# Setup of a graph and expert kernel: half-size row buffers, column sums on two engines, scaling on the way out of PSUM

## The reference

```python
def _L0_gnn_ref(H, W, A):
    HW = einsum('bnf,fo->bno', H, W)
    A_norm = relu((A + A.T) * 0.5)
    D = sum(A_norm, axis=1)
    D_safe = where(D > 0, D, 1.0)
    d_inv_sqrt = where(D > 0, D_safe ** (-0.5), 0.0)
    DAD = d_inv_sqrt[:, None] * A_norm * d_inv_sqrt[None, :]
    L_norm = eye(N) - DAD
    return relu(einsum('nm,bmo->bno', L_norm, HW))

x = x + _L0_gnn_ref(_layernorm(x, axis=-1), L0_gnn_W, adj)
x = x + _L0_ffn_ref(_layernorm(x, axis=-1), router_w, w1, b1, w2, b2)
```

## Time and profile before

| | |
|---|---|
| median of 3 runs | 950.52 us |
| profiled execution, its own time | 949.63 us |
| its span | 947.9 us |
| TensorE busy, share of the span | 94% |
| VectorE | 68% |
| ScalarE | 55% |
| GpSimd | 33% |
| granted TensorE clock, mean | 0.986 of full |
| HBM traffic over the span | 235 GB/s |

### The profile page before, as it was taken

The page is one execution under the profiler, slowest core; times in us unless marked ns, Lnnn a source line. Parts: engine busy times, 40 slices in busy tenths (PEclk is TensorE's granted clock), DMA queues, the critical chain, the costliest instruction groups (busy, mean ns, idle before and its releaser), DMA issues.

```text
span 947.9 us, 15352 instructions
## 1 busy us (share of the span) xinstructions
PE 890.9 (94%) x4446; PEld 724.9 (76%) x4446; DVE 645.9 (68%) x1558; ACT 516.9 (55%) x899; POOL 311.3 (33%) x312
## 2 busy tenths in 40 slices
PE   4766799999999999999999989999999999999997
PEld 3765588888888788878888857777777777777775
DVE  3996634756867734152424288888888888888886
ACT  3665332344443321222122287888888888888885
POOL 0689335555574734474433430000000000000000
PEclk9997899999999999999999999999999999999999
DMA  9983255676485336867766774777777777777771
GB/s 286 327 253 125 98 202 212 255 270 215 166 290 175 102 139 251 281 245 262 267 246 239 286 253 163 263 265 266 267 269 270 270 270 270 270 270 270 270 269 45
DMA packets 93022, 222.98 MB, mean 235 GB/s; under 512 B 8856, under 2 KB 59568, under 8 KB 81072
## 3 DMA queue, kind: packets, MB, share of 16 engines
q1 hardware_dynamic: 86752, 211.59, 63.3%
q0 software_dynamic: 2560, 8.39, 2.3%
q10 hardware_dynamic: 3664, 2.43, 1.0%
HBM read 157.89 MB, written 64.49 MB: 235 GB/s over the span
## 4 chain that ended last, share of the span: by engine, by line
PE 81%; DVE 7%; POOL 4%; issue 4%; ACT 3%; DMA 1%; DVEq 0%; ACTq 0%; POOLq 0%
PE bank L913 11%; PE bank L915 11%; PE bank L914 11%; PE bank L1290 6%; PE bank L1293 6%; PE bank L1277 6%; PE bank L1279 6%; PE bank L1278 6%; PE bank L1291 6%; POOL col_sum L543 3%; PE bank L858 2%; PE bank L330 2%; DVE y_lo L699 2%; PE bank L1299 1%; PE bank L1287 1%
## 5 line engine op out<-in xcount | busy, mean ns | idle before, releaser
L1367 DVE TENSOR_TENSOR gated<-c_all,act_h 128x512 f32<-128x512 f32 x256 | 177.7, 694 | 46.2 <-ACT act_h L1329 41.6
L1329 ACT ACTIVATE act_h<-bank,b_sb 128x512 f32<-128x512 f32 x256 | 176.5, 690 | 58.5 <-PE bank L1279 54.0
L1372 DVE TENSOR_TENSOR g_lo<-gated,g_hi 128x512 fp32r<-128x512 f32 x256 | 175.7, 686 | 0.2
L1336 ACT ACTIVATE g_hi<-gated 128x512 fp32r<-128x512 f32 x256 | 159.1, 621 | 4.4 <-DVE gated L1367 4.4
L1262 POOL DMA_DIRECT2D out<-fin x32 | 24.3, 759 | 367.6 <-DVE fin L1380 362.9
L913 PE MATMUL bank<-y_hi,stage 128*128 128x512 f32 x256 | 111.3, 435 | 3.6 <-DVE y_lo L699 3.6
L1002 POOL TENSOR_TENSOR rstd<-var_eps,neg_half 128x4 f32<-128x4 f32 x32 | 48.8, 1525 | 179.5 <-DVE var_eps L1039 179.4
L1277 PE MATMUL bank<-z_e,w_hi 128*128 128x512 f32 x256 | 103.8, 406 | 1.7 <-ACT act_h L1329 1.5
L913 PE MATMUL bank<-y,stage 128*128 128x512 f32 x256 | 104.5, 408 | 0.0
L1293 PE MATMUL bank<-g_lo,w_hi 128*128 128x512 f32 x256 | 101.0, 395 | 2.9 <-DVE g_lo L1372 2.9
L1290 PE MATMUL bank<-g_hi,w_lo 128*128 128x512 f32 x256 | 103.7, 405 | 0.0
(11 more groups left out here) (118 smaller groups left out, 1582.1 us busy)
## 6 DMA issues: line engine op xcount, KB each, us to landing
c_all<-c_scratch SPq DMA_DIRECT2D x64, 1024.0 KB, 8.0
s_scratch<-stage SPq DMA_DIRECT2D x14, 2048.0 KB, 8.4
stage<-s_scratch SPq DMA_DIRECT2D x14, 2048.0 KB, 7.8
z_e<-z_scratch SPq DMA_DIRECT2D x32, 512.0 KB, 7.0
z_scratch<-z_hl SPq DMA_DIRECT2D x31, 512.0 KB, 2.7
x_raw<-in_x SPq DMA_DIRECT2D x32, 256.0 KB, 7.8
x_res<-in_x SPq DMA_DIRECT2D x32, 256.0 KB, 7.1
r_e<-res_scratch SPq DMA_DIRECT2D x32, 256.0 KB, 2.7
```

The costliest lines, as they stand in the source:

```text
L1329: act.activation(v.act_h[e % R][:, :], ps_h[e % 2][:, :], ACT.Gelu, bias=v.b1_sb[:, e:e + 1]).then_inc(gelu_done, 1)
L1336: act.activation(v.g_hi[e % R][:, :], v.gated[e % R][:, :], ACT.Copy).then_inc(hi_done, 1)
L1367: dve.tensor_tensor(out=v.gated[e % R][:, :], in0=v.c_all[s][:, e, :], in1=v.act_h[e % R][:, :], op=ALU.mult).then_inc(gated_done, 1)
L1372: dve.tensor_tensor(out=v.g_lo[e % R][:, :], in0=v.gated[e % R][:, :], in1=v.g_hi[e % R][:, :].bitcast(FP32), op=ALU.subtract).then_inc(lo ...
```

## The change

1. **Buffers.** The last eight steps use half-size buffers: each of the three sets is cut in two, so that there are six for steps 8 to 15. `FREED_BY` names the step whose sum frees a buffer. Before, the load of step 11 waited for the sum of step 8, that of step 15 for the sum of step 13; now they wait for the sums of steps 6 and 9.
2. **Column sums.** GpSimd adds rows down to j = 5 only. The rows 4 to 1 enter a column's sum as more products with the column of ones on TensorE. Each of the three parts of the degrees has its own PSUM bank.
3. **Projections.** Jobs 0 to 3 are kept and scaled as before, but in steps 0 to 2. From job 4 on, ScalarE scales on the way out of PSUM, four 128x128 pieces a job, each with its own scale. The power -0.5 is taken for each step's jobs. Two PSUM banks take turns for the projections of the first half, and ScalarE does `keep` behind the relus of a step, not ahead of them.
4. **Variance.** `x_var` is made by a TENSOR_REDUCE over the variance and a constant in a third column, where a TENSOR_SCALAR was.
5. **Order at the end.** The first four `y_high`/`y_low` (m = 15 to 12) go into steps 14 and 15. The staging of unit 1's row goes between the remaining ones, ahead of the graph stage. Its four turned groups stand behind blocks 4, 7, 11 and 14 of unit 0, where they stood behind 2, 4, 10 and 13.

```diff
-    ps_x, ps_p = v.banks[4], v.banks[5]
+    ps_x, ps_p = v.banks[4], [v.banks[5] if k % 2 or k >= v.MB else v.banks[3] for k in range(v.U)]
...
-        dve.tensor_scalar(v.x_var[:, k, :], v.x_mv[:, :, 1], v.EPS, None, ALU.add).then_inc(x_var_done, 1)
+        dve.tensor_reduce(out=v.x_var[:, k, :], in_=v.x_mv[:, :, 1:3], axis=AX.X, op=ALU.add).then_inc(x_var_done, 1)
...
-        elif k <= MB:
+        elif k < MB:
+            wait(pe, hw_kept, k - 1)
+        elif k == MB:
             pe.wait_ge(hw_kept, k)
...
     def keep(act, k):
         _, m = place(k)
         act.wait_ge(hw_done, k + 1)
-        act.activation(v.hw0[:, m, :], ps_p[:, :], ACT.Copy).then_inc(hw_kept, 1)
+        if k < KEPT_RAW:
+            act.activation(v.hw0[:, m, :], ps_p[k][:, :], ACT.Copy).then_inc(hw_kept, 1)
+        else:
+            act.wait_ge(x_rstd_done, k + 1)
+            for q in range(Q):
+                last = act.activation(v.hw0[:, m, q * P:(q + 1) * P], ps_p[k][:, q * P:(q + 1) * P], ACT.Identity,
+                                      scale=v.x_rstd[:, k, q:q + 1])
+            last.then_inc(hw_kept, 1)
...
-    SET = [r % 3 if r < 12 else 1 + r % 2 for r in range(MB)]
+    SET = [r % 3 if r < 8 else 3 + (r - 8) % 6 for r in range(MB)]
+    HALVES = [(2, 0), (2, 1), (0, 0), (0, 1), (1, 0), (1, 1)]
+    FREED_BY = [None, None, None, 0, 1, 2, 3, 4, 5, 5, 6, 6, 7, 7, 8, 9]
+    low = low + [v.low[i][:, h * N // 2:(h + 1) * N // 2] for i, h in HALVES]
+    up = up + [v.up[i][:, h * MB // 2:h * MB // 2 + MB // 2 - 1, :] for i, h in HALVES]
...
+    LAST = 5
+    EARLY_AT = ((15, 14), (13, 12))
+    EARLY = 4
+    SECOND_AT = (7, 5, 3, 0)
...
-    ps_d = v.banks[7]
+    ps_d = [v.banks[2], v.banks[7], v.banks[4]]
...
         for r, j in enumerate(ROWS):
-            if 1 <= j <= MB - 2:
+            if r < 4:
+                pr.invert(pool, jobs(r))
+            for k in jobs(r - 1):
+                if k < pr.KEPT_RAW:
+                    pr.scale_kept(pool, k)
+            if 4 <= r < 12:
+                pr.invert(pool, jobs(r))
+            if LAST <= j <= MB - 2:
                 add_columns(j)
-            if r in (2, 4, 8, 12):
-                first = 4 * (2, 4, 8, 12).index(r)
-                pr.invert(pool, range(first, first + 4))
-            if r == 9:
+            if r == 10:
                 root(0)
-            if r in (10, 11, 12, 13):
-                for k in range(2 * (r - 10), 2 * (r - 10) + 2):
-                    pr.scale_kept(pool, k)
             if r == 14:
                 root(1)
         root(2)
-        for k in range(8, MB):
-            pr.scale_kept(pool, k)
...
+            for k in jobs(r):
                 if k:
                     pr.keep(act, k - 1)
-            for g in range(n_groups(j)):
-                relu(r, j, g)
...
+            if r >= 14:
+                for m in EARLY_AT[r - 14]:
+                    y_high(m)
-        for m in range(MB - 1, -1, -1):
+        for m in range(MB - 1 - EARLY, -1, -1):
             y_high(m)
+            if m == 10:
+                st.high_direct(act, 1)
+            if m in SECOND_AT:
+                st.high_group(act, 1, SECOND_AT.index(m))
...
             if k <= MB - 3:
-                pe.wait_ge(col_added, 14 - k)
+                pe.wait_ge(col_added, 14 - max(k, LAST - 1))
...
+            for j in range(LAST - 1, k, -1):
+                if j == k + 1:
+                    pe.wait_ge(relued, until_row(j))
+                last = pe.matmul(out, s_tri[:, block(j, k), :], v.one_col[:, :], start=False, stop=(j == k + 1))
...
-            if ahead and i in S_AT and S_AT.index(i) < st.n_groups(u + 1):
-                st.turn_group(pe, u + 1, S_AT.index(i))
+            s_at = S_AT if u else (4, 7, 11, 14)
+            if ahead and i in s_at and s_at.index(i) < st.n_groups(u + 1):
+                st.turn_group(pe, u + 1, s_at.index(i))
```

More of the change, by code:

```diff
@@ L364, in project_program @@
     pr.scale_kept, pr.scale_by_d, pr.turn_x, pr.copy_x, pr.project = scale_kept, scale_by_d, turn_x, copy_x, project
-    pr.keep, pr.scale, pr.high, pr.low = keep, scale, high, low
+    pr.keep, pr.scale, pr.high, pr.low, pr.wait_scaled = keep, scale, high, low, wait_scaled
     return pr
@@ L451, in setup_stage @@
 def setup_stage(nc, sem, v):
-    E, MB, CW, Q = v.E, v.MB, v.CW, v.Q
+    E, MB, CW, Q, N = v.E, v.MB, v.CW, v.Q, v.N
     low, up, s_tri, ident = v.low, v.up, v.s_tri, v.ident
-    low_in = [sem(f"low_in{i}") for i in range(3)]
-    up_in = [sem(f"up_in{i}") for i in range(3)]
+    low_in = [sem(f"low_in{i}") for i in range(9)]
+    up_in = [sem(f"up_in{i}") for i in range(9)]
     consts_made = sem("consts_made")
@@ L511, in sync @@
             s = SET[r]
-            before = [i for i in range(r) if SET[i] == s]
             for k in jobs(r):
                 pr.load(sp, k)
-            if before:
-                sp.wait_ge(summed, first_group[before[-1] + 1])
+            if r >= 3:
+                sp.wait_ge(summed, first_group[FREED_BY[r] + 1])
             sp.dma_start(low[s][:, 0:(j + 1) * P], v.adj[j * P:(j + 1) * P, 0:(j + 1) * P]).then_inc(low_in[s], 16)
@@ L592, in scalar @@
                 pr.copy_x(act, k)
+            for g in range(n_groups(j)):
+                relu(r, j, g)
+            for k in jobs(r):
                 if k:
                     pr.keep(act, k - 1)
-            for g in range(n_groups(j)):
-                relu(r, j, g)
             if r == 12:
@@ L683, in degrees @@
             dve.wait_ge(col_done, MB - a)
-            dve.tensor_tensor(out=v.deg_raw[:, a:b], in0=ps_d[:, a:b], in1=v.deg_row[:, a:b], op=ALU.add).then_inc(deg_step, 1)
+            dve.tensor_tensor(out=v.deg_raw[:, a:b], in0=ps_d[p][:, a:b], in1=v.deg_row[:, a:b], op=ALU.add).then_inc(deg_step, 1)
             dve.wait_ge(deg_step, first + 2)
@@ L720, in vector @@
                 degrees(1)
+            if r >= 14:
+                for m in EARLY_AT[r - 14]:
+                    y_low(m)
         degrees(2)
-        for m in range(MB - 1, 2, -1):
+        for m in range(MB - 1 - EARLY, -1, -1):
             y_low(m)
-        outward()
-        for m in range(2, -1, -1):
-            y_low(m)
+            if m == 10:
+                st.diagonal(dve, 1)
+                st.low_direct(dve, 1)
+            if m in SECOND_AT:
+                st.low_group(dve, 1, SECOND_AT.index(m))
+            if m == 3:
+                outward()
     stage = Plan()
@@ L974, in scalar @@
                 evict(u - 1)
-            if ahead:
+            if ahead and u:
                 st.high_direct(act, u + 1)
@@ L984, in scalar @@
                         copy_gate(w)
-                if ahead and g < st.n_groups(u + 1):
+                if u and ahead and g < st.n_groups(u + 1):
                     st.high_group(act, u + 1, g)
@@ L1111, in vector @@
                 mid(u - 1)
-            if ahead:
-                if u == 0:
-                    st.diagonal(dve, 1)
+            if ahead and u:
                 st.low_direct(dve, u + 1)
             for g in range(4):
-                if ahead and g < st.n_groups(u + 1):
+                if u and ahead and g < st.n_groups(u + 1):
                     st.low_group(dve, u + 1, g)
```

37 lines of the change are left out of this document (23 added, 14 removed).

## The result

The changed kernel takes 940.19 us (median of 4 runs, 935.79 to 941.07) against 950.07 of before in the same runs (948.55 to 951.11): ratio 0.9888 [0.9854, 0.9922], so it is 10 us faster. The forecast was 935.5. The profiled execution has 940.29 us for its own time and a span of 938.6; the forecast's sum for it was 935.0, so 5.3 us are missing.

A forecast was written before the change was run, and what follows sets the result against it. Unit 1's start bounds the kernel: TensorE is gapless behind it. Moving it from 112.4 to 97.8 us (6.4 earlier start, 8.2 shorter unit 0) takes 14.6 off 949.6: 935.0, stated 935.5; own range 930.5 to 938.5, with rivals to 942.

The forecast's parts named there:

- The frame: From unit 1's start on, TensorE works without a gap, so whatever moves that start moves the end by as much.
- GpSimd late for job 15: Rival in setup: GpSimd's nine powers at 1.6 us each delay job 15, +3.5 us, 939 us; chance 0.13.
- a low clock all through unit 0: Rival in unit 0: TensorE's clock stays low throughout, 7.1 us more, 942.5 us; chance 0.09.
- The load order is the same and DMA is full, so the transposes of step 10 stay at 63.8 us: Setup up to step 10: TensorE's transposes start no later than before, at 63.8 us.
- TensorE's added column sums run in its idle time: Setup: column sums moved from GpSimd to TensorE cost no time; unit 0 starts at 81.5 instead of 87.86 us.
- Steps 11 to 15: End of setup: sums of steps 11 and 12 start at 68.8 instead of 71.29 us; last relu at 81.4.
- x_var: VectorE's variance in setup: 0.18 us as a TENSOR_REDUCE, where it took 1.70 at 61.57 us.
- The low parts' pace: VectorE's low parts: 0.69 us each instead of 1.14, since GpSimd has nothing left to do.
- The stop: TensorE's 5.06 us stop in unit 0, waiting for unit 1's staging, goes; counted in the 8.2 us from unit 0's length.
- Unit 0's length: Unit 0 takes 16.3 us instead of 24.5, a gain of 8.2 us.
- The half-size buffers: Loads of rows 11 to 13 land earlier, worth 1.2 us; rival that nothing is gained: 936.7 us, inside the own range.
- the pace: Rival in setup: GpSimd's powers at nearly 3.00 us add 17 us to its line, kernel slower at 952 us; chance 0.04.

The follow-up runs named there:

- e3_last3: The changed kernel with GpSimd summing rows down to j = 3 instead of 5: 936.19 us, ratio 0.9850.
- e1_keep_ahead: The changed kernel with ScalarE keeping the projections ahead of a step's relus again: 938.24 us, ratio 0.9877.
- e2_raw8: The changed kernel with jobs 0 to 7 kept unscaled ahead of the relus and GpSimd scaling jobs 4 to 7 in step 12: 937.54 us.
- e12_after_last1: The changed kernel with GpSimd summing the columns of all rows and TensorE adding none: 935.92 us, ratio 0.9854.
- e10_x_var: The kernel combining e2_raw8 and e3_last3, with the variance made by a TENSOR_SCALAR again: 938.88 us, ratio 0.9895.
- e9_raw16: The kernel combining e2_raw8 and e3_last3, with jobs 8 to 15 also kept unscaled and scaled by GpSimd behind its last root: 938.38 us.
- e8_late_staging: The kernel combining e2_raw8 and e3_last3, with all high and low parts behind the rows and unit 1 staged in unit 0 again: 937.94 us.
- e4_old_sets: The changed kernel with the old three full-size buffer sets in all 16 steps: 940.14 us, ratio 0.9903.

## Why the prediction was right or wrong

The frame, the sign and the range (930.5 to 942) held; the forecast's own range, up to 938.5, did not. That the range held is in part luck: it reached to 942 for two rivals, GpSimd late for job 15 and a low clock all through unit 0, and neither came; what took the 4.7 us between forecast and median was none of the rivals that I had named. The gain by place is wrong too. Of the 14.6 us forecast, 6.4 were to come from unit 0's earlier start, and nothing did (87.86 us before, 87.92 now); 8.2 were to come from its length, and 9.0 did. Of the signs named for a right forecast, the first product near 81.5 and the eviction at 97 to 99 us failed. Two steps failed, and together they are the missing 5.3 us.

- **"The load order is the same and DMA is full, so the transposes of step 10 stay at 63.8 us": failed, +3.3 us in the profiled execution.** I priced the keeps behind the relus as ScalarE's time (0.4 us each, "hides under the loads") and not as a wait for TensorE. `project` of a job waits for the `keep` of two jobs before, and the transposes of the step are queued behind it. In the two-job steps that `keep` stands behind the relus of the step before. TensorE stops for about 2 us each time, the buffers come free late, the loads fall back, and the low clock decides how much of it shows (67.09, 65.68, and 63.64 us in e3_last3). Why the clock is low in one execution and full in the next stays open. By the medians, putting the keeps ahead again gave 2.0 us (e1_keep_ahead), e2_raw8 2.7.
- **"TensorE's added column sums run in its idle time": failed, +2.8 us at the first product.** TensorE had no idle time there: the ten products, each two records of L679 and 0.43 us in all, come on the 0.50 clock and run between 80.99 and 87.92 us, beside the transposes and the sums that it had before. Without them (e12_after_last1) the first product comes 2.55 us earlier, and 1.36 us of that reach the eviction.
- **Steps 11 to 15: right, shifted.** Sums of steps 11 and 12 at 72.34 (forecast 68.8), staging of unit 0 at 76.58 (72.8), sum of step 14 at 81.44 (77.7), last relu at 85.10 (81.4): 3.5 to 3.8 us late each, of which 3.3 is step 10. Four pieces of `keep` took 1.12 us, not 0.9, and the held `deg_none` 1.09.
- **x_var: right.** 0.16 us (forecast 0.18), and worth 3.0 us of the kernel's time (e10_x_var; priced at 2.5). But of the 3.8 us that e10_x_var is late at the sums of step 11, 1.6 arise ahead of step 10, where I had seen nothing to gain; that the two prices agree is in part luck.
- **The low parts' pace: right.** 0.69 us each, worth 2.5 us net (e9_raw16). Where GpSimd scales beside them they take 1.47. **The stop:** 5.06 us are gone; the reordering is worth 2.1 (e8_late_staging): the stop is only 1.63 us once the low parts are fast, and the rest is the later first product.
- **Unit 0's length: right.** 15.5 us from the first product to unit 1 (forecast 16.3). The clock was low for 3.6 us of it and then full.
- **The half-size buffers: the price is not settled.** I gave them 1.2 us. e4_old_sets shows none in the time, and 2.3 up to the last relu, which the clock under the column sums gave back.
- **The rivals.** GpSimd was neither late nor the pace: the powers are eight of one job at 1.00 to 1.03 us, not nine, and one of two jobs at 1.65. Its sum of row 5 did end behind 70 us (at 72.6), one of my signs of being wrong, but the late step 10 had moved it. The clock rose inside unit 0; its low stretch did its harm ahead of it, in the column sums and in steps 3 and 4, where I had not looked.

Two slips of the working change nothing: 80.9 + 15.2 is 96.1 and not 96.3, and 935.0 + 0.9 is 935.9 where I said 935.5.

Summed for the profiled execution, with 98.0 us for the forecast's eviction (0.2 behind unit 1's start): step 10 +3.3, from there to the last relu +0.4, column sums +2.7 (the forecast had 0.1 between the last relu and the first product), unit 0 -0.8: 5.6 us, which is the distance from 98.0 to 103.58. Later 0.3 came back, and 5.3 are missing in the time.

## What to carry to other kernels

When an instruction is moved behind others on its engine, price the wait of whoever needs its result, and list what stands behind that waiter on its own engine: a copy that itself costs nothing where it stands held back the transposes, and with them the loads, of a stage bound by DMA. Work handed to an engine that "has idle time" must be costed at that engine's granted clock and in its place in the order; here the helper had itself been relieved by the same change, and did not need the help. If a kernel's runs spread more than those of its neighbours, look for short waits of TensorE on a low clock: the kernels here without the three waits spread over 2.3 us at most, those with them over 2.7 to 6.3. And before you call a part worthless because taking it out costs no time, look whether something else gave the time back, as the clock did in e4_old_sets.
